# Two gathered tiles of each round, instead of one, fetched row by row by SyncE from byte offsets

## The chip, the core and the metric

One core of a Trainium2 chip. TensorE multiplies matrices, VectorE, ScalarE and GpSimd compute and copy, SyncE computes nothing and issues DMA transfers. The metric is the time of one execution on the device, in microseconds, median of the runs.

## The reference

A graph network layer on 12,500 nodes (128 values each) and 400,000 edges, sorted by their destination:

```python
h_nodes = mlp2(x);  h_edges = mlp2(edge_attr)                 # 64 wide
msg_in  = concatenate([h_nodes[dst], h_nodes[src], h_edges])  # per edge
msgs    = silu(msg_in @ msg_W1 + msg_b1) @ msg_W2 + msg_b2
agg     = segment_sum(msgs, dst) / maximum(counts, 1)
out     = layernorm(x + x + mlp2(concatenate([x, agg])))      # two norms in all
```

The part that matters here is `h_nodes[src]`: for each edge one row of 64 floats, at an index that the input gives.

## The kernel before

A first stage computes two tables of node rows in DRAM, `a_table` (the part of the first message layer that belongs to destinations) and `b_table` (sources), 256 bytes a row. It also keeps the nodes' hidden layer on chip (`nT`).

Then come 625 **units** of 640 edges, each 5 tiles of 128 edges. 25 units make a **round**, and there are 25 rounds; all of it is written out as straight code. For each unit TensorE adds up the first message layer in `p_pre`: `second_layer` (L696: edge part and destination part, against the window of `a_table` in `wa_ring`), then `source_term` (L702 adds the gathered rows in `b_ring`; L705 computes a tile from `colbuf`). ScalarE applies Silu, TensorE sums messages into a window of nodes (`window_sums`, L716), VectorE adds that to `agg`.

The source rows come in three ways. In 12 of the 25 units (`SPECIAL`) the fifth tile isn't gathered: VectorE and ScalarE copy 128 columns of `nT` into `colbuf` (L642), from lists of byte offsets made on chip (`column_bytes`, stored to DRAM by `store_column_bytes` and read back in pieces). GpSimd gathers the others with one indirect DMA for each tile of 128 rows (`pool_gathers`, L834), up to `BLAG` = 8 units ahead of TensorE: 112 tiles a round. The last tile is SyncE's: tile 3 of unit 24 (`ROW_TILE`), 128 transfers of one row each (`fetch_rows`, L763), 8 in each of units 7 to 22. For these SyncE loads 8 row numbers into registers (L758) from `row_list`, which is read from an input, and uses each as an index into `b_table`, an array of 4-byte floats 64 wide. Unit 24 has a slot of its own in `b_ring` (`b_slot`).

SyncE's program is `sync_units`, one queue in strict order. For unit i: at the first unit of a chunk (units 0, 5, 9, 13, 17, 21) a wait on `second_mm`, two edge loads (L809) and one of destinations (L811); the start of the unit's window, loaded 4 words at a time (`next_start`, L564); a wait for `second_mm`; the window of `a_table` (L815); at units 8 and 21 the column lists (L735); then the rows; then the loads and the store of the node update of the round before (L973, L974, L978). `second_mm` counts the units whose second layer is done, plus `LEAD` = 5, so that

```python
wait_alone(eng, second_mm, r * ROUND + i + 1)
```

lets SyncE go past the window of unit i when TensorE has finished the second layer of unit i - 5. TensorE needs a chunk's edges for `hidden_mm` (L849), which runs three units ahead: after the second layer of unit i it multiplies the edges of unit i + 3. It waits for the rows of unit 24 before that unit's source term.

Of the kernel before, what the change touches and what calls it, by code (L numbers as in the profile page):

```python
# [5 lines left out]
F32, I32, U8 = mybir.dt.float32, mybir.dt.int32, mybir.dt.uint8  # L6
ALU, ACT, AX = mybir.AluOpType, mybir.ActivationFunctionType, mybir.AxisListType
ds = bass.ds

P = 128  # L10
H = 64
D = 128
W = 64
TILES = 5
UE = TILES * P
HALF = UE // 2
ROUND = 25
# [22 lines left out]
LIST_AT = (21, 8)  # L40
LOAD = dict(vector=32, scalar=40)
LISTED = 656
ROW_TILE = (24, 3)
ROWS_A_STEP = 8
ROWS_FROM = 7
WORDS = 4

AT = dict(load=0, ready=2, count=3, mean=4, up=5, hidden=6, down=7, sum=8, norm1=9, affine=10, sum2=11, norm2=12,
# [10 lines left out]
def program(nc, a, out, stack):  # L59
# [25 lines left out]

    a_table = nc.dram_tensor("a_table", (NPAD, H), F32, kind="Internal").ap()
    b_table = nc.dram_tensor("b_table", (N, H), F32, kind="Internal").ap()
    byte_list = {who: nc.dram_tensor("bytes_for_" + who, (LISTED * LOAD[who],), I32, kind="Internal").ap() for who in COLS}
    assert all(LISTED >= UNITS + LEADIN + ROUND and LISTED * LOAD[who] % P == 0 for who in COLS)
    agg = sb("agg", [P, NPAD], F32)  # L90

# [39 lines left out]
    b_ring = sb("b_ring", [P, BRING, TILES, H], F32)  # L131
    wa_ring = sb("wa_ring", [P, RING, H], F32)
    hot_ring = sb("hot_ring", [P, HOTS, TILES, W], F32)
    all_cols = hot_ring[:, :, :, :].rearrange("p s t w -> p (s t w)").bitcast(I32)[:, 0:sum(LISTED * LOAD[who] // P for who in COLS)]
    comb = sb("comb", [P, COMBS, UE], F32)
    msg = sb("msg", [P, 2, TILES, H + 1], F32)
    work = sb("work", [P, 8 * BANK], F32)
# [8 lines left out]
    for who in COLS:  # L146
# [1 line left out]
        lists[who] = to_ab[0:1, :, :, :, :].rearrange("o s t q n -> o (s t q n)").bitcast(I32)[:, at:at + words]\  # L148
            .rearrange("o (k n) -> o k n", n=LOAD[who])
        at += words  # L150
    row_list = to_ab[0:1, :, :, :, :].rearrange("o s t q n -> o (s t q n)").bitcast(I32)[:, at:at + P]
    assert at + P <= SR * 2 * 2 * GJ * H
    pad = sb("pad", [W, H], F32)
    rows = e_ring[0:1, :, :].rearrange("p s c -> p (s c)")
    startf, ahead = rows[:, 0:UNITS], rows[:, UNITS:2 * UNITS]
# [190 lines left out]
    def scalar_nodes(eng):  # L346
        for to, of in first_fold:
            eng.dma_start(to, of).then_inc(s_wf, 16)
        eng.wait_ge(s_bx, 32)
        for k in range(PAIRS):  # L350
            if k < PAIRS:
                _, gs, n = pair_of[k]
                eng.wait_ge(s_h, k + 1)
                if k >= SR:
                    eng.wait_ge(s_ab, k - SR + 1)
                eng.activation(n1[k % SR][0:gs * H, 0:n].rearrange("k (j p) -> k j p", j=GJ),
                               p_hid[0:gs * H, k % 2, 0:n].rearrange("k (p j) -> k j p", j=GJ),
                               ACT.Silu, bias=b_n1[0:gs * H, :]).then_inc(s_n1, 1)
                first, _, _ = pair_of[k]
                for g in range(gs):  # L360
                    last = eng.activation(nT[:, first + g * n:first + (g + 1) * n], p_hid[g * H:(g + 1) * H, k % 2, 0:n],
                                          ACT.Silu, bias=b_n1[g * H:(g + 1) * H, :])
                last.then_inc(s_nt, 1)
            if k < len(fold_loads):
                to, of = fold_loads[k]
                eng.dma_start(to, of).then_inc(s_w, 16)
            if k == 5:
                eng.dma_start(dst[:, :], a["dst"]).then_inc(s_dst, 16)
            if k == PAIRS - 2:
                for who, words in column_parts():  # L370
                    eng.dma_start(words, a["cols_" + who]).then_inc(s_cols, 16)
        for to, of in later_loads:
            eng.dma_start(to, of).then_inc(s_w2, 16)

# [63 lines left out]
    def vector_nodes(eng):  # L438
# [21 lines left out]
            eng.tensor_copy(startf[:, :], first).then_inc(s_sf, 1)  # L460

        def column_bytes():
            eng.wait_ge(s_cols, 16 * len(COLS))
            eng.tensor_scalar(all_cols, all_cols, 4, None, ALU.mult).then_inc(s_byte, 1)

        def window_spread():

# [126 lines left out]
    def b_slot(i):  # L594
        return i % BLAG if i < ROUND - 1 else BLAG

    def gathered(i):

        return [k for k in range(TILES) if not (i in SPECIAL and k == TILES - 1)]

    def by_pool(i):

        return [k for k in gathered(i) if (i, k) != ROW_TILE]

    def b_value(r, i):

# [35 lines left out]
            end = copy(colbuf[:, special % COLBUF, at:at + 1].bitcast(U8), of[j])  # L642
        return end

    def column_parts():

        at = 0
        for who in COLS:
            words = LISTED * LOAD[who] // P
            yield who, all_cols[:, at:at + words]  # L650
            at += words

    def store_column_bytes(eng):
        eng.wait_ge(s_byte, 1)
        for who, words in column_parts():
            eng.dma_start(byte_list[who].rearrange("(p c) -> p c", p=P), words).then_inc(s_stl, 16)

    def a_value(r, i):
# [78 lines left out]

    def sync_first(eng):

        eng.wait_ge(s_stl, 16 * len(COLS))  # L740
        a_table_stored(eng)
        for i in range(SR):
            eng.wait_ge(s_stb[i], 16 * stores(PAIRS, i))
        load_list(eng, 0, 0, LEADIN, lead_in)
        load_list(eng, LEADIN, LEADIN, HALF_AT, list_in[0])

        load_rows(eng, 0)

    def load_rows(eng, r):

        eng.dma_start(row_list, a["rows"][ds(r * P, P)].unsqueeze(0)).then_inc(row_list_in, 16)

    def fetch_rows(eng, r, i):

        first = (i - ROWS_FROM) * ROWS_A_STEP
        if first == 0:
            wait_alone(eng, row_list_in, 16 * r + 16)
        _, nodes = nc.values_load_multi_w_load_instructions(  # L758
            row_list[:, first:first + ROWS_A_STEP], engines=[eng.engine], min_val=0, max_val=N - 1,
            skip_runtime_bounds_check_because="an edge's source is a node")  # L760
        unit, tile = ROW_TILE
        for q, node in enumerate(nodes):
            eng.dma_start(b_ring[first + q:first + q + 1, b_slot(unit), tile, :], b_table[ds(node, 1), :])\  # L763
               .then_inc(row_in[q % len(row_in)], 16)
        if first + ROWS_A_STEP == P:
            load_rows(eng, r + 1)

    def sync_last(eng):
# [28 lines left out]
    def sync_units(eng, base, n, step):  # L797
        for k in range(n):
            r, i = place(base, k)
            c, at = chunk_of(i)  # L800
            if at == 0:
                n = CHUNKS[c]
                first = r * (ROUND * UE) + i * UE
                here = slice(spot(i), spot(i) + n)

                wait_alone(eng, second_mm, r * ROUND + i + LEAD - CHUNKS[c - 1])
                cols = a["edgeT"][:, ds(first, n * UE)].rearrange("k (u c) -> k u c", c=UE)
                for part in range(2):
                    eng.dma_start(e_ring[part * H:(part + 1) * H, here, :], cols[:, :, part * HALF:(part + 1) * HALF])\  # L809
                       .then_inc(e_in[c % 2], 16)  # L810
                eng.dma_start(dst_ring[:, here, :].rearrange("p u c -> p (u c)"),  # L811
                              a["dst_row"][ds(first, n * UE)].partition_broadcast(H)).then_inc(d_in[c % 2], 16)
            start = next_start(eng, r, i)
            wait_alone(eng, second_mm, r * ROUND + i + 1)
            eng.dma_start(wa_ring[H:P, i % RING, :], a_table[ds(start, W), :]).then_inc(a_in[i % RING], 16)  # L815
            if i in LIST_AT:
                half = LIST_AT.index(i)
                copied = r * ROUND + LEADIN + (HALF_AT if half == 0 else 0)
                chunk, n = ((r + 1) * ROUND, HALF_AT) if half == 0 else (r * ROUND + HALF_AT, ROUND - HALF_AT)
                wait_alone(eng, col_ok["vector"], copied)  # L820
                wait_alone(eng, col_ok["scalar"], copied)
                load_list(eng, chunk + LEADIN, LEADIN + half * HALF_AT, n, list_in[half])
            if 0 <= i - ROWS_FROM < P // ROWS_A_STEP:
                fetch_rows(eng, r, i)
            step(k)

    def pool_gathers(eng, units):
# [24 lines left out]
    def tensor_units(eng, r, n, step):  # L852
# [14 lines left out]
        for i in range(n):  # L867
# [14 lines left out]
            if j in SPECIAL and i < ADD_LAG + 1:  # L882
                for who in COLS:
                    wait_alone(eng, col_ok[who], cols_value(who, rr, j))
            if j == ROW_TILE[0]:
                for arrived in row_in:
                    wait_alone(eng, arrived, (rr + 1) * (16 * P // len(row_in)))
            eng.wait_ge(b_in[b_slot(j)], b_value(rr, j))
            source_term(eng, i, j, b_slot(j)).then_inc(pre_mm, 1)
            step(i)  # L890
# [260 lines left out]
    with nc.Block() as block:  # L1151
# [34 lines left out]
        @block.vector  # L1186
        def _(eng):
            vector_nodes(eng)
            eng.sem_inc(sum_ok, 1)
            eng.sem_inc(gen["done"], 1)  # L1190
            eng.wait_ge(s_pool, 5)
            eng.wait_ge(s_stl, 16 * len(COLS))
            choose(eng, vector_first, vector_units, vector_general, vector_updates, vector_last)

def _laid_out(inputs):
# [9 lines left out]
    for k in ("src", "dst"):  # L1206
        d[k] = g[k].reshape(-1, P).T
    d["dst_row"] = g["dst"].reshape(-1)
    rows = g["src"].reshape(-1, ROUND, TILES, P)[:, ROW_TILE[0], ROW_TILE[1], :]
    d["rows"] = np.concatenate([rows, np.zeros_like(rows[0:1])]).reshape(-1)  # L1210
    special = g["src"].reshape(-1, ROUND, TILES, P)[:, SPECIAL, TILES - 1, :]
    chunks = special.shape[0] * ROUND
    for who, (first, last) in dict(vector=(0, COLS["vector"]), scalar=(COLS["vector"], P)).items():
# [2 lines left out]
        listed = np.zeros((LISTED, LOAD[who]), part.dtype)  # L1216
        for k in range(chunks):
            listed[k, 0:at[k + 1] - at[k]] = part[at[k]:at[k + 1]]
        d["cols_" + who] = listed.reshape(P, -1)
    return {k: np.ascontiguousarray(t) for k, t in d.items()}  # L1220

# [12 lines left out]
```

## Time and profile before

| | |
|---|---|
| time, median of 3 runs | 4890.29 us (4887.94 to 4896.6) |
| span of the profiled execution | 3612.0 us |
| median less span | 1278.3 us |
| units, from the first window load on SyncE to the last | 76 to 3552 us |
| GpSimd busy | 2674.4 us (74%) |
| ScalarE busy | 2994.3 us (83%) |
| TensorE matmuls busy | 2874.1 us (80%) |
| VectorE busy | 2737.3 us (76%) |

The page gives the profiled execution by its span from the first to the last instruction; the time of the runs holds 1278.3 us more, which the trace doesn't cover, so that a change in the span is set on the median as it is. A round takes (3552 - 76) / 25 = 139 us. Busy time doesn't hold what an engine's queue does with registers, loads into registers and issues of DMAs; SyncE has no busy time at all, and is read from its queue's instructions.

### The profile page before, as it was taken

What the parts mean: (1) busy time and instruction counts of PE and PEld (TensorE: products, weight loads), DVE (VectorE), ACT (ScalarE), POOL (GpSimd) and SP (SyncE); (2) the same over time, 40 slices, a digit from 0 to 9 for tenths busy, and PEclk for the clock granted to TensorE, in tenths of its full rate; (3) what the DMA queues carried; (4) which work ended last, traced back from release to release, by engine and by line L of the source; (5) the groups of instructions that cost most, each with busy time, mean ns of one, the idle gap of its engine ahead of it and who ended that gap; (6) DMA issues with size and microseconds to landing.
All of it is one profiled execution on the core that took longest, in us unless ns stands there. A gap on an engine that the chain in (4) does not pass through costs nothing.

```text
span 3612.0 us, 103943 instructions
## 1 busy us (share of the span) xinstructions
PE 2874.1 (80%) x16224; PEld 2219.4 (61%) x16224; DVE 2737.3 (76%) x20847; ACT 2994.3 (83%) x23073; POOL 2674.4 (74%) x2823
## 2 busy tenths in 40 slices
PE   4878888877878878888778888777778878877885
PEld 2666666666666666666666666656665656656664
DVE  4777778778777777777787777787777777877876
ACT  4998888888887888988888888888878888888785
POOL 4777777777777777777777777777777777777773
PEclk7687777677777777777777777777777776677766
DMA  7454444454444454444454444444444444444441
GB/s 225 78 113 100 87 94 100 89 102 96 95 95 86 96 102 90 101 100 88 93 103 85 102 96 95 99 95 87 98 92 99 101 89 96 90 92 102 96 95 43
DMA packets 263059, 350.77 MB, mean 97 GB/s; under 512 B 111714, under 2 KB 199121, under 8 KB 252514
## 3 DMA queue, kind: packets, MB, share of 16 engines
q1 hardware_dynamic: 169792, 246.77, 32.0%
q0 software_dynamic: 90624, 95.15, 14.5%
q14 instruction: 558, 4.57, 0.5%
q8 instruction: 131, 2.15, 0.3%
q10 hardware_dynamic: 1954, 2.14, 0.2%
HBM read 330.78 MB, written 13.01 MB: 95 GB/s over the span
## 4 chain that ended last, share of the span: by engine, by line
POOL 62%; issue 21%; PE 8%; DMA 4%; DVE 4%; DVEq 0%; ACT 0%; SPq 0%; ACTq 0%; POOLq 0%
POOL b_ring L834 62%; DMA b_ring<-b_table,src 4%; PE p_pre L696 2%; PE p_pre L702 1%; DVE colbuf L642 1%; PE p_sum L716 1%; PE p_hid L849 1%; DVE comb L939 1%; DMA work<-in_xT 1%; PE p_pre L705 0%; PE p_last L995 0%; PE p_last L996 0%; DVEq L627 0%; DVE stats L1032 0%; ACT colbuf L642 0%
## 5 line engine op out<-in xcount | busy, mean ns | idle before, releaser
L834 POOL DMA_INDIRECT b_ring<-b_table,src x2800 | 2652.0, 947 | 858.9 <-issue 844.8
L642 ACT COPY colbuf<-shared 64x4 uint8 x21134 | 2127.4, 190 | 159.9 <-issue 148.4
L642 DVE COPY colbuf<-shared 64x4 uint8 x17511 | 1377.6, 194 | 308.6 <-issue 301.9
L696 PE MATMUL p_pre<-wa_ring,comb 128*128 128x64 f32 x6250 | 1047.1, 329 | 0.0
L696 PEld LDWEIGHTS p_pre<-wa_ring,comb 128*128 128x128 f32 x6250 | 996.8, 245 | 0.9 <-issue 0.8
L727 ACT ACTIVATE comb<-p_hid,b_e 64x320 f32<-64x320 f32 x1250 | 652.8, 522 | 360.4 <-PE p_hid L849 350.9
L939 DVE SCALAR_TENSOR_TENSOR comb<-shared,p_const 64x640 f32<-64x640 int32 x625 | 554.0, 887 | 458.8 <-PE p_pre L696 336.2
L716 PEld LDWEIGHTS p_sum<-hot_ring,msg 128*65 128x65 f32 x6250 | 589.2, 181 | 500.0 <-DVE agg L949 265.0
L716 PE MATMUL p_sum<-hot_ring,msg 128*65 128x64 f32 x6250 | 649.5, 269 | 291.1 <-DVE agg L949 166.6
L702 PE MATMUL p_pre<-b_ring,ident 128*128 128x320 f32 (+1 forms) x1250 | 583.4, 559 | 341.4 <-DMA b_ring<-b_table,src 340.8
L849 PE MATMUL p_hid<-e_ring,w_e 128*128 128x320 f32 x1250 | 626.2, 591 | 49.0 <-DMA e_ring<-in_edgeT 40.0
L702 PEld LDWEIGHTS p_pre<-b_ring,ident 128*128 128x128 f32 x1250 | 302.1, 255 | 559.7 <-DMA b_ring<-b_table,src 439.9
L928 DVE TENSOR_TENSOR hot_ring<-dst,p_const 128x320 f32<-128x320 f32 x625 | 304.7, 487 | 19.7
L721 ACT ACTIVATE msg<-p_pre 128x320 f32<-128x320 f32 x625 | 273.6, 438 | 22.8 <-PE p_pre L702 12.8
L849 PEld LDWEIGHTS p_hid<-e_ring,w_e 128*128 128x128 f32 x1250 | 245.9, 244 | 54.3 <-DMA e_ring<-in_edgeT 44.1
L705 PEld LDWEIGHTS p_pre<-w_ab,colbuf 64*128 64x128 f32 x600 | 111.6, 232 | 137.4 <-issue 137.4
L705 PE MATMUL p_pre<-w_ab,colbuf 64*128 64x64 f32 x600 | 158.6, 353 | 0.0
L949 DVE TENSOR_TENSOR agg<-agg,p_sum 65x64 f32 x625 | 135.4, 217 | 9.0 <-issue 3.4
L1022 DVE RECIPROCAL p_last<-p_last 64x500 f32<-64x500 f32 x25 | 82.1, 3282 | 0.9
L1001 PEld LDWEIGHTS p_last<-w_u,work 65*125 65x125 f32 x200 | 49.1, 321 | 6.1 <-ACT work L1006 2.4
L995 PE MATMUL p_last<-work,w_ux 128*64 128x500 f32 x50 | 45.8, 1016 | 5.3 <-DVE work L1024 5.3
L1001 PE MATMUL p_last<-w_u,work 65*125 65x128 f32 x200 | 47.6, 388 | 0.8 <-ACT work L1006 0.8
(106 smaller groups left out, 599.2 us busy)
## 6 DMA issues: line engine op xcount, KB each, us to landing
e_ring<-in_edgeT SPq DMA_DIRECT2D x250, 320.0 KB
shared<-in_dst_row SPq DMA_DIRECT2D x125, 640.0 KB
b_ring<-b_table SPq DMA_DIRECT2D x3200, 0.2 KB
b_ring<-b_table,src POOLq DMA_INDIRECT x2800
e_ring<-in_edgeT SPq DMA_DIRECT2D x50, 400.0 KB
shared<-in_dst_row SPq DMA_DIRECT2D x25, 800.0 KB
wa_ring<-a_table SPq DMA_DIRECT2D x625, 16.0 KB
work<-in_xT SPq DMA_DIRECT2D x25, 250.0 KB
```

Source lines behind the costliest of these rows:

```text
L642: end = copy(colbuf[:, special % COLBUF, at:at + 1].bitcast(U8), of[j])
L696: return eng.matmul(p_pre[:, i % 2, k * H:(k + 1) * H], comb[:, i % COMBS, k * P:(k + 1) * P], wa_ring[:, i % RING, :], start=k == 0, stop ...
L702: last = eng.matmul(p_pre[:, i % 2, 0:n * H], ident[:, :], b_ring[:, slot, 0:n, :].rearrange("p k n -> p (k n)"), start=False, stop=n == T ...
L705: last = eng.matmul(p_pre[:, i % 2, n * H:(n + 1) * H], colbuf[:, SPECIAL.index(j) % COLBUF, :], w_ab[0:H, H:2 * H], start=False, stop=True)
L716: last = eng.matmul(sums_of(i), msg[:, i % 2, k, :], hot_ring[:, i % HOTS, k, :], start=k == 0, stop=k == TILES - 1)
L721: return eng.activation(msg[:, i % 2, :, 0:H], of, ACT.Silu)
L727: last = eng.activation(comb[0:H, i % COMBS, part * HALF:(part + 1) * HALF], p_hid[rows, bank, 0:HALF], ACT.Silu, bias=b_e1[rows, :])
L834: eng.indirect_dma_start(b_ring[:, b_slot(i), k, :], None, b_table, bass.IndirectOffsetOnAxis(ap=src[:, u * TILES + k:u * TILES + k + 1], ...
L849: eng.matmul(p_hid[:, i % 2, 0:HALF], w_e1[:, :], e_ring[:, spot(j), :], start=True, stop=True)\
L928: eng.tensor_tensor(hot_ring[:, i % HOTS, :, :], dst[:, ds((base + i) * TILES, TILES)].bitcast(F32).unsqueeze(2).to_broadcast([P, TILES, W ...
L939: eng.scalar_tensor_tensor(comb[H:P, i % COMBS, :], dst_ring[:, spot(j), :], win_from[:, ds(base + i, 1)], p_row.to_broadcast([H, UE]), AL ...
L949: eng.tensor_tensor(window, window, sums_of(i), ALU.add).then_inc(sum_ok, 1)
```

## The change

Tile 2 of unit 24 is fetched by SyncE too (`ROW_TILES`), so GpSimd gathers 111 tiles a round instead of 112. SyncE fetches 256 rows a round: 12 in each of units 5 to 20, 16 in each of units 21 to 24. Their offsets come as bytes: the list of row numbers is multiplied by 256 on VectorE in the first stage, together with the column lists, stored to DRAM and read back 256 words a round. The source of a transfer is now a slice of `b_table` seen as single bytes. The loads into registers (now 12 or 16 words) stand ahead of the wait for `second_mm` instead of behind the window's load.

```diff
-ROW_TILE = (24, 3)
-ROWS_A_STEP = 8
-ROWS_FROM = 7
+ROW_TILES = [(24, 2), (24, 3)]
+ROWS = P * len(ROW_TILES)
+ROWS_FROM = 5
+ROWS_A_STEP = [12] * 16 + [16] * 4
...
+            eng.tensor_scalar(all_lists[:, columns:], all_lists[:, columns:], 4 * H, None, ALU.mult).then_inc(s_byte, 1)
...
-        return [k for k in gathered(i) if (i, k) != ROW_TILE]
+        return [k for k in gathered(i) if (i, k) not in ROW_TILES]
...
-        eng.dma_start(row_list, a["rows"][ds(r * P, P)].unsqueeze(0)).then_inc(row_list_in, 16)
-
-    def fetch_rows(eng, r, i):
-
-        first = (i - ROWS_FROM) * ROWS_A_STEP
+        eng.dma_start(row_list, byte_list["rows"][ds(r * ROWS, ROWS)].unsqueeze(0)).then_inc(row_list_in, 16)
+
+    def row_numbers(eng, r, i):
+
+        k = i - ROWS_FROM
+        first, n = sum(ROWS_A_STEP[0:k]), ROWS_A_STEP[k]
         if first == 0:
             wait_alone(eng, row_list_in, 16 * r + 16)
-        _, nodes = nc.values_load_multi_w_load_instructions(
-            row_list[:, first:first + ROWS_A_STEP], engines=[eng.engine], min_val=0, max_val=N - 1,
+        _, starts = nc.values_load_multi_w_load_instructions(
+            row_list[:, first:first + n], engines=[eng.engine], min_val=0, max_val=4 * H * (N - 1),
             skip_runtime_bounds_check_because="an edge's source is a node")
-        unit, tile = ROW_TILE
-        for q, node in enumerate(nodes):
-            eng.dma_start(b_ring[first + q:first + q + 1, b_slot(unit), tile, :], b_table[ds(node, 1), :])\
+        return starts
+
+    def fetch_rows(eng, r, i, starts):
+
+        first = sum(ROWS_A_STEP[0:i - ROWS_FROM])
+        for q, start in enumerate(starts):
+            which, row = divmod(first + q, P)
+            unit, tile = ROW_TILES[which]
+            eng.dma_start(b_ring[row:row + 1, b_slot(unit), tile, :].bitcast(U8), b_bytes[ds(start, 4 * H)].unsqueeze(0))\
                .then_inc(row_in[q % len(row_in)], 16)
-        if first + ROWS_A_STEP == P:
+        if first + len(starts) == ROWS:
             load_rows(eng, r + 1)
...
             start = next_start(eng, r, i)
+            fetches = 0 <= i - ROWS_FROM < len(ROWS_A_STEP)
+            starts = row_numbers(eng, r, i) if fetches else None
             wait_alone(eng, second_mm, r * ROUND + i + 1)
```

## Rows read from the trace of the kernel before

**Rows 1.** The page: its head and the busy time of the engines.
```profile
span 3612.0 us, 103943 instructions
...
PE 2874.1 (80%) x16224; PEld 2219.4 (61%) x16224; DVE 2737.3 (76%) x20847; ACT 2994.3 (83%) x23073; POOL 2674.4 (74%) x2823
```
**Rows 2.** The page's costliest groups: GpSimd's gathers.
```profile
L834 POOL DMA_INDIRECT b_ring<-b_table,src x2800 | 2652.0, 947 | 858.9 <-issue 844.8
```
**Rows 3.** Who waited for whom: us in total, times, longest us.
```profile
POOL b_ring L834 <- issue: 844.8, 2772, 0.3
...
PE p_pre L702 <- DMA b_ring<-b_table,src: 340.8, 141, 6.6
...
PE p_hid L849 <- DMA e_ring<-in_edgeT: 40.0, 25, 11.7
...
POOL b_ring L834 <- PE p_pre L705: 5.2, 17, 0.3
```
**Rows 4.** The same for SyncE's queue.
```profile
SPq L815 <- PE p_pre L696: 755.6, 229, 12.7
SPq L558 <- PE p_pre L696: 88.4, 23, 6.2
```
**Rows 5.** Single lines on SyncE: duration in ns, min/median/max, first and last start.
```profile
L763 SPq FUSED_REGOPS  x3200: 37/37/42, 104.8 to 3545.1; - x189
L763 SPq MOVE b_ring<-b_table x3200: 29/29/38, 104.9 to 3545.1; - x189
L763 SPq DMA_DIRECT2D b_ring<-b_table x3200: 217/225/327, 105.0 to 3545.2; - x189
...
L758 SPq TENSOR_LOAD <-to_ab x400: 524/962/983, 104.3 to 3541.2; - x134
...
L564 SPq TENSOR_LOAD <-win_start x157: 303/603/1697, 75.4 to 3547.0; - x157
...
L815 SPq DMA_DIRECT2D wa_ring<-a_table x625: 468/486/547, 76.4 to 3551.9; - x157
```
**Rows 6.** A single line on VectorE's queue: the load of 28 words into registers.
```profile
L627 DVEq TENSOR_LOAD <-to_ab x633: 850/1850/3725, 73.6 to 3570.5; - x159
```
**Rows 7.** SyncE's timeline, cut to four row transfers, then two units (start, us, what).
```profile
1131.06 1.45 SPq L763 DMA_DIRECT2D b_ring<-b_table  x4
...
1129.79 3.13 SPq L763 DMA_DIRECT2D b_ring<-b_table  x8
1133.10 0.49 SPq L815 DMA_DIRECT2D wa_ring<-a_table  x1
...
1134.76 3.12 SPq L763 DMA_DIRECT2D b_ring<-b_table  x8
```
**Rows 8.** The timelines of SyncE and TensorE around the chunk of unit 13.
```profile
2502.70 1.33 SPq L809 DMA_DIRECT2D e_ring<-in_edgeT  x2
2504.07 0.61 SPq L811 DMA_DIRECT2D shared<-in_dst_row  x1
...
2508.41 0.81 PE L849 MATMUL p_hid<-e_ring,w_e 128*128 128x320 f32 x2
```
**Rows 9.** TensorE's timeline: second layers of units 22, 24, 25; two, elsewhere, apart.
```profile
2578.37 2.32 PE L696 MATMUL p_pre<-wa_ring,comb 128*128 128x64 f32 x10
...
2589.64 1.28 PE L696 MATMUL p_pre<-wa_ring,comb 128*128 128x64 f32 x10
...
2592.51 1.28 PE L696 MATMUL p_pre<-wa_ring,comb 128*128 128x64 f32 x10
...
695.57 2.34 PE L696 MATMUL p_pre<-wa_ring,comb 128*128 128x64 f32 x10
...
701.64 2.34 PE L696 MATMUL p_pre<-wa_ring,comb 128*128 128x64 f32 x10
```
**Rows 10.** SyncE's timeline: the shortest and a long one of the other issues.
```profile
1017.22 0.24 SPq L751 DMA_DIRECT2D to_ab<-in_rows  x1
...
1051.15 0.58 SPq L973 DMA_DIRECT2D work<-in_xT  x1
```

More of the change, by code:

```diff
@@ L87, in program @@
     b_table = nc.dram_tensor("b_table", (N, H), F32, kind="Internal").ap()
-    byte_list = {who: nc.dram_tensor("bytes_for_" + who, (LISTED * LOAD[who],), I32, kind="Internal").ap() for who in COLS}
+    byte_list = {"rows": nc.dram_tensor("bytes_for_rows", ((E // UE // ROUND + 1) * ROWS,), I32, kind="Internal").ap()}
+    byte_list |= {who: nc.dram_tensor("bytes_for_" + who, (LISTED * LOAD[who],), I32, kind="Internal").ap() for who in COLS}
     assert all(LISTED >= UNITS + LEADIN + ROUND and LISTED * LOAD[who] % P == 0 for who in COLS)
@@ L133, in program @@
     hot_ring = sb("hot_ring", [P, HOTS, TILES, W], F32)
-    all_cols = hot_ring[:, :, :, :].rearrange("p s t w -> p (s t w)").bitcast(I32)[:, 0:sum(LISTED * LOAD[who] // P for who in COLS)]
+    listed = {who: LISTED * LOAD[who] // P for who in COLS} | {"rows": (ROUNDS + 1) * ROWS // P}
+    all_lists = hot_ring[:, :, :, :].rearrange("p s t w -> p (s t w)").bitcast(I32)[:, 0:sum(listed.values())]
+    assert sum(ROWS_A_STEP) == ROWS and ROWS_FROM + len(ROWS_A_STEP) <= ROUND
+    b_bytes = b_table.rearrange("n h -> (n h)").bitcast(U8)
     comb = sb("comb", [P, COMBS, UE], F32)
@@ L150, in program @@
         at += words
-    row_list = to_ab[0:1, :, :, :, :].rearrange("o s t q n -> o (s t q n)").bitcast(I32)[:, at:at + P]
-    assert at + P <= SR * 2 * 2 * GJ * H
+    row_list = to_ab[0:1, :, :, :, :].rearrange("o s t q n -> o (s t q n)").bitcast(I32)[:, at:at + ROWS]
+    assert at + ROWS <= SR * 2 * 2 * GJ * H
     pad = sb("pad", [W, H], F32)
@@ L369, in scalar_nodes @@
             if k == PAIRS - 2:
-                for who, words in column_parts():
-                    eng.dma_start(words, a["cols_" + who]).then_inc(s_cols, 16)
+                for who, words in list_parts():
+                    eng.dma_start(words, a["list_" + who]).then_inc(s_cols, 16)
         for to, of in later_loads:
@@ L462, in column_bytes @@
         def column_bytes():
-            eng.wait_ge(s_cols, 16 * len(COLS))
-            eng.tensor_scalar(all_cols, all_cols, 4, None, ALU.mult).then_inc(s_byte, 1)
+            eng.wait_ge(s_cols, 16 * len(listed))
+            columns = sum(listed[who] for who in COLS)
+            eng.tensor_scalar(all_lists[:, 0:columns], all_lists[:, 0:columns], 4, None, ALU.mult).then_inc(s_byte, 1)
+            eng.tensor_scalar(all_lists[:, columns:], all_lists[:, columns:], 4 * H, None, ALU.mult).then_inc(s_byte, 1)
         def window_spread():
@@ L643, in copied_columns, with list_parts @@
         return end
-    def column_parts():
+    def list_parts():
         at = 0
-        for who in COLS:
-            words = LISTED * LOAD[who] // P
-            yield who, all_cols[:, at:at + words]
+        for who, words in listed.items():
+            yield who, all_lists[:, at:at + words]
             at += words
     def store_column_bytes(eng):
-        eng.wait_ge(s_byte, 1)
-        for who, words in column_parts():
+        eng.wait_ge(s_byte, 2)
+        for who, words in list_parts():
             eng.dma_start(byte_list[who].rearrange("(p c) -> p c", p=P), words).then_inc(s_stl, 16)
@@ L738, in sync_first @@
     def sync_first(eng):
-        eng.wait_ge(s_stl, 16 * len(COLS))
+        eng.wait_ge(s_stl, 16 * len(listed))
         a_table_stored(eng)
@@ L822, in sync_units @@
                 load_list(eng, chunk + LEADIN, LEADIN + half * HALF_AT, n, list_in[half])
-            if 0 <= i - ROWS_FROM < P // ROWS_A_STEP:
-                fetch_rows(eng, r, i)
+            if fetches:
+                fetch_rows(eng, r, i, starts)
             step(k)
@@ L884, in tensor_units @@
                     wait_alone(eng, col_ok[who], cols_value(who, rr, j))
-            if j == ROW_TILE[0]:
+            if j == ROW_TILES[0][0]:
                 for arrived in row_in:
-                    wait_alone(eng, arrived, (rr + 1) * (16 * P // len(row_in)))
+                    wait_alone(eng, arrived, (rr + 1) * (16 * ROWS // len(row_in)))
             eng.wait_ge(b_in[b_slot(j)], b_value(rr, j))
@@ L1191, in _ @@
             eng.wait_ge(s_pool, 5)
-            eng.wait_ge(s_stl, 16 * len(COLS))
+            eng.wait_ge(s_stl, 16 * len(listed))
             choose(eng, vector_first, vector_units, vector_general, vector_updates, vector_last)
@@ L1208, in _laid_out @@
     d["dst_row"] = g["dst"].reshape(-1)
-    rows = g["src"].reshape(-1, ROUND, TILES, P)[:, ROW_TILE[0], ROW_TILE[1], :]
-    d["rows"] = np.concatenate([rows, np.zeros_like(rows[0:1])]).reshape(-1)
+    tiles = g["src"].reshape(-1, ROUND, TILES, P)
+    rows = np.concatenate([tiles[:, unit, tile, :] for unit, tile in ROW_TILES], axis=1)
+    d["list_rows"] = np.concatenate([rows, np.zeros_like(rows[0:1])]).reshape(P, -1)
     special = g["src"].reshape(-1, ROUND, TILES, P)[:, SPECIAL, TILES - 1, :]
@@ L1218, in _laid_out @@
             listed[k, 0:at[k + 1] - at[k]] = part[at[k]:at[k + 1]]
-        d["cols_" + who] = listed.reshape(P, -1)
+        d["list_" + who] = listed.reshape(P, -1)
     return {k: np.ascontiguousarray(t) for k, t in d.items()}
```

## The prediction

> **What bounds the kernel now.** I read the page first. No engine is busy above 83% [rows 1], so busy shares don't name the bound. The costliest groups do: GpSimd's 2800 gathers are busy for 2652.0 us, and 844.8 us of idle time lie between them, all put down to issue [rows 2]. Each gather so takes (2652.0 + 844.8) / 2800 = 1.249 us, and 112 of them make 139.9 us, the whole round. The waits confirm it: of the 2800, GpSimd waited 17 times for the last product of a unit, 5.2 us in total, while TensorE waited 340.8 us for gathered tiles [rows 3]. GpSimd never stops, and the others follow it.
>
> Then I looked at the engine that gets the work. SyncE waits for TensorE at L815 in only 229 of 625 units, 755.6 us, and 88.4 us at L558 [rows 4]. Of the 3476 us from its first to its last window load it is thus occupied for 3476 - 844 = 2632 us, 105.3 us of each round, and it has 34.6 us to spare. In 396 units it finds its condition met, that is, it comes late; the two neighbouring units of the timeline begin their rows 4.97 us apart [rows 7] without any slack, where GpSimd's pace is 139.9 / 25 = 5.60 us a unit.
>
> **What the change takes from GpSimd.** One gather a round: 1.249 us, 25 times, 31 us. A round on GpSimd alone would be 111 x 1.249 = 138.6 us. This is all that can be gained.
>
> **What one row costs on SyncE.** Four transfers in a run end 1.45 us after the first begins; less the last one's 0.225 us, the pitch is 1.225 / 3 = 0.408 us [rows 5, 7]. It holds three instructions: FUSED_REGOPS 37 ns, MOVE 29 ns, the transfer 225 ns; 117 ns are left, three gaps of 39 ns. Bounds: 0.254 us if all the gaps went with it, 0.371 us if only the 37 ns go, 0.408 us if nothing does. Rows a round: 128 x 0.408 = 52.2 us now, 256 x 0.332 = 85.0 us after.
>
> The Trainium skill ("DMA: Bandwidth & Descriptors", section "Anatomy of one DMA") gives about 50 ns for the dispatch of a DMA by the sequencer; the trace has 225 ns. By the page's figure, estimated, a row would cost 0.157 us, SyncE would keep up, and the change would be worth its 31 us.
>
> **What the loads into registers cost.** Eight words take 962 ns in the median and 524 ns at least [rows 5]; 28 words on VectorE take 1850 ns [rows 6]. That is 0.044 to 0.066 us for each further word. Some loads will stand right behind another one and be short. I take 1.10 us for 12 words and 1.35 us for 16, with a gap of 0.04 us: 1.14 and 1.39 us. Bounds: 0.524 us (no growth) and 1.85 us. Their place ahead of the wait hides them only where SyncE waits.
>
> **SyncE's sum alone.** Now 105.3; less 52.2 for rows and 16 x 1.00 for loads; plus 85.0, 16 x 1.14 and 4 x 1.39: 145.9 us. Already this is above 139.9.
>
> **The chain of one round.** SyncE can't spread this sum over the round. In units 0 to 4 it has no rows and is soon held by `second_mm`. So I follow it from the moment when TensorE's second layer of unit 0 lets it past the wait of unit 5:
> - 256 rows: 85.0
> - loads, 15 of 12 words (that of unit 5 lies ahead of the wait) and 4 of 16: 17.1 + 5.6 = 22.7
> - 20 window loads, each 486 + 29 + 37 ns and three gaps of 40: 13.4
> - the chunks of units 9, 13, 17, 21 and of the next unit 0, each 2.02 (1.98 from first to last, and a gap) [rows 8]: 10.1
> - 5 loads of window starts of 0.603 + 0.04 [rows 5]: 3.2
> - eight short issues (four of column lists, one of offsets, three of the node update), 0.24 to 0.58 us each [rows 10], about 0.38 with the gap: 3.0
>
> Together 137.4 us, back to back. 20 units of GpSimd's pace are 112 us, so SyncE falls behind by 25 us. What is late next is the chunk of the next unit 0: TensorE needs its edges three units ahead, right after the second layer of unit 22, and VectorE its destinations. They land 3.7 us after the last issue: in the trace the product with new edges starts at 2508.41, SyncE's issues end at 2504.68 [rows 8], and this is an upper bound there. Then TensorE has to do units 23, 24 and 0 up to the second layer before SyncE is let past the wait of unit 5 again: 2592.51 - 2578.37 = 14.1 us for three such steps [rows 9]. Bounds: 3 x 2.87 = 8.6 us at the pace of the last step of these, 3 x 6.07 = 18.2 us at that of the slow pair. The release itself is 0.2 us.
>
> Round: 137.4 + 3.7 + 14.1 + 0.2 = 155.4 us, against 139.9: 15.5 us more, 25 times, 387 us. The span becomes about 4000 us; the 1278 us around it stay, and the median 4890 becomes 5277 us.
>
> Free, and why: the offsets' product on VectorE and one more list to store are under 1 us once, beside two stores of the same kind. The rows of unit 24 are issued before the late chunk, and TensorE needs them almost two units after it. Slots: eight units of GpSimd's lead are 45 us, more than the 25 us by which TensorE falls behind, so GpSimd only waits.
>
> **The rivals.**
> - *GpSimd stays the bound (the other side).* If SyncE's chain fits in 138.6 us, the round shrinks by 1.25 us: 4859 us. This decides at one price, the pitch: 0.332 - 16.8 / 256 = 0.266 us. For it: three gaps might shrink together, and the bound of 0.254 lies below. Against: it wants MOVE or the transfer shorter as well, and the transfer's 217 to 225 ns hardly vary [rows 5]. 10%; a pitch near 0.271 would give no change, 3%.
> - *SyncE bounds by its sum only.* If the light units hid what I charge for landing and for TensorE's three steps, the round is 145.9 us: +150 us, 5040 us. For it: TensorE comes through 2.87 us steps. Against: the wait at L815 is in the code. 9%.
> - *Loads don't grow with their words.* 19 of them at 0.524 + 0.04 make 10.7 instead of 22.7 us: round 143.4, +88 us, 4978 us. Against: 1850 ns for 28 words [rows 6]. 5%. The Trainium skill (same page, "Latency and other measured facts") gives a floor of some 600 ns for such a load, amortized by taking several words. At 0.64 us each, an estimate, the round would be 144.9 us and the time 5015 us; the trace's 962 ns speaks against it.
> - *Byte transfers save nothing.* At 0.408 the round is 155.4 + 19.5 = 174.9 us: 5765 us; at 0.371, 5527 us. For it: no transfer of single bytes from DRAM is in this trace. Against: FUSED_REGOPS only stands where an index is multiplied. 7%.
>
> **How the numbers follow.** The forecast has 66%: 5277 us, by TensorE's bounds 5140 to 5380, so with its own range 5100 to 5420. The range for 8 in 10 takes in the second and third rival and leaves out the first and the last (10 + 3 + 7 = 20%): 4980 to 5480. Faster by over 0.2% (10 us, about what a measurement tells from no change) 10%, within it 3%, slower 87%.
>
> **What the changed profile would show.** No FUSED_REGOPS at the line of the rows, and runs of transfers with a pitch of 0.33 us. Loads of about 1.1 and 1.35 us. SyncE waiting in three or four units a round, those without rows, instead of nine. GpSimd no longer without waits: 25 x (155.4 - 138.6) = 420 us behind the last product of a unit. TensorE waiting for edges or VectorE for destinations once a round, near unit 22, for 10 us or more. Wrong it would be with a pitch below 0.27 us, with GpSimd still at 1.249 us without waits, or with a stall in another place: rows of unit 24 that come last, or a chunk in the middle of the rows.

## The result, and the profile after

The changed kernel took 5552.77 us (5546.78 to 5558.01, 4 runs) against 4889.11 us, a ratio of 1.1365 (95% interval 1.1338 to 1.1392): 664 us slower, where 387 were forecast, and outside the range.

The page of the changed kernel shows at once what the forecast had missed. Its head, the engines' busy time, the gathers:

```profile
span 5549.8 us, 107221 instructions
...
PE 3422.5 (62%) x16224; PEld 2655.8 (48%) x16224; DVE 2933.4 (53%) x20848; ACT 3124.7 (56%) x23073; POOL 2662.0 (48%) x2798
...
L849 POOL DMA_INDIRECT b_ring<-b_table,src x2775 | 2639.6, 951 | 2772.0 <-PE p_pre L708 1456.4
```

This execution's own time is 5551.7 us: span and time differ by 2 us, and so they did in every later run of either kernel. So 1278 us of "time around the span" never existed. The page of the kernel before, with 3612 us [rows 1], must have come from an execution that was itself some 1276 us shorter than the timed ones. All runs since then fall on two levels, and each set of runs, made one after the other, has only one of them: the medians of the kernel before are 3611 to 3614 us in some sets and 4884 to 4952 us in others, with nothing between. The first comparison was made at the longer level, its forecast from a profile of the shorter one. I call the two conditions A (about 3611 us) and B (about 4900 us) from here on. They aren't two kinds of chip, though the expectations below speak so: the sets recorded under chip number 10 were in A at first, in B 20 minutes later, and in A again after that.

What B does shows most plainly on SyncE's queue. Single lines on it in the changed kernel in B (duration min/median/max in ns), and two runs of 12 rows among many from its timeline:

```profile
L776 SPq MOVE b_ring<-b_table x6400: 2/29/1422, 129.6 to 5510.6; - x194
L776 SPq DMA_DIRECT2D b_ring<-b_table x6400: 3/225/963, 129.7 to 5510.7; - x194
...
2589.06 3.91 SPq L776 DMA_DIRECT2D b_ring<-b_table  x12
...
2594.76 7.10 SPq L776 DMA_DIRECT2D b_ring<-b_table  x12
```

FUSED_REGOPS is gone from the line of the rows, as forecast, and the medians of the rest are those of [rows 5]. But a MOVE that took 29 to 38 ns now takes between 2 and 1422 ns, and of two runs of 12 transfers one takes 3.91 us and the next 7.10. The queue is held up, mostly for 0.6 to 0.8 us at a time, and then does a few instructions in a few ns each.

The same kernel in A, with nothing held up: single lines, the queue's waits, GpSimd's wait.

```profile
L776 SPq MOVE b_ring<-b_table x6400: 29/29/38, 100.2 to 4039.8; - x194
L776 SPq DMA_DIRECT2D b_ring<-b_table x6400: 217/225/433, 100.3 to 4039.8; - x194
...
L765 SPq TENSOR_LOAD <-to_ab x500: 748/1013/3137, 87.0 to 4032.8; - x167
...
SPq L830 <- PE p_pre L702: 311.5, 65, 11.8
...
POOL b_ring L849 <- PE p_pre L708: 461.4, 91, 14.2
```

Here it took 4080.5 us against 3613.4 (ratio 1.1294, 1.127 to 1.1317): 467 us slower. SyncE waits at L830 in 65 units of 625 instead of 229 [rows 4], GpSimd waits 461 us for the product at L708, where its waits for the last product of a unit had been 5.2 us in all [rows 3].

### The profile page after: what moved, and what is told of

Read it like the earlier page. It is cut to its first block, busy times and chain, and to the rows that moved or that the text cites. A ratio compares the mean times of both kernels' runs of the same rounds, so it can differ in the third digit from the quotient of the medians.

```text
span 5549.8 us, 107221 instructions
## 1 busy us (share of the span) xinstructions
PE 3422.5 (62%) x16224; PEld 2655.8 (48%) x16224; DVE 2933.4 (53%) x20848; ACT 3124.7 (56%) x23073; POOL 2662.0 (48%) x2798
## 4 chain that ended last, share of the span: by engine, by line
SPq 54%; issue 30%; DVE 6%; DMA 4%; PE 3%; another core or an unknown queue 2%; DVEq 1%; ACT 0%; ACTq 0%
SPq L776 36%; SPq L765 7%; SPq L830 5%; DVE colbuf L649 4%; DMA shared<-in_dst_row 3%; SPq L822 2%; DVE comb L954 1%; PE p_pre L702 1%; SPq L571 1%; SPq L824 1%; DMA e_ring<-in_edgeT 1%; PE p_sum L722 1%; DVEq L634 1%; SPq L741 0%
## 5 line engine op out<-in xcount | busy, mean ns | idle before, releaser
L649 ACT COPY colbuf<-shared 64x4 uint8 x21134 | 2252.0, 190 | 821.6 <-issue 801.8
L649 DVE COPY colbuf<-shared 64x4 uint8 x17511 | 1533.3, 193 | 974.8 <-issue 964.8
L864 PE MATMUL p_hid<-e_ring,w_e 128*128 128x320 f32 x1250 | 768.0, 712 | 1025.0 <-DMA e_ring<-in_edgeT 988.8
L722 PE MATMUL p_sum<-hot_ring,msg 128*65 128x64 f32 x6250 | 750.7, 296 | 1043.6 <-DVE agg L964 423.4
L722 PEld LDWEIGHTS p_sum<-hot_ring,msg 128*65 128x65 f32 x6250 | 672.3, 206 | 1330.7 <-DVE agg L964 833.5
L702 PE MATMUL p_pre<-wa_ring,comb 128*128 128x64 f32 x6250 | 1277.3, 380 | 0.0
L702 PEld LDWEIGHTS p_pre<-wa_ring,comb 128*128 128x128 f32 x6250 | 1224.7, 294 | 1.0 <-issue 1.0
L864 PEld LDWEIGHTS p_hid<-e_ring,w_e 128*128 128x128 f32 x1250 | 295.1, 291 | 1048.6 <-DMA e_ring<-in_edgeT 1010.9
L708 PE MATMUL p_pre<-b_ring,ident 128*128 128x320 f32 (+1 forms) x1250 | 653.2, 621 | 1.0 <-DMA b_ring<-b_table 1.0
L708 PEld LDWEIGHTS p_pre<-b_ring,ident 128*128 128x128 f32 x1250 | 373.8, 299 | 208.1 <-issue 182.6
```

The source lines that it names most:

```text
L702: return eng.matmul(p_pre[:, i % 2, k * H:(k + 1) * H], comb[:, i % COMBS, k * P:(k + 1) * P], wa_ring[:, i % RING, :], start=k == 0, stop ...
L708: last = eng.matmul(p_pre[:, i % 2, 0:n * H], ident[:, :], b_ring[:, slot, 0:n, :].rearrange("p k n -> p (k n)"), start=False, stop=n == T ...
L722: last = eng.matmul(sums_of(i), msg[:, i % 2, k, :], hot_ring[:, i % HOTS, k, :], start=k == 0, stop=k == TILES - 1)
L864: eng.matmul(p_hid[:, i % 2, 0:HALF], w_e1[:, :], e_ring[:, spot(j), :], start=True, stop=True)\
```

## The experiments

**The kernel before, again, and the two halves of the change apart.** `one_tile_bytes` sets, in the changed kernel,

```diff
-ROW_TILES = [(24, 2), (24, 3)]
-ROWS_FROM = 5
-ROWS_A_STEP = [12] * 16 + [16] * 4
+ROW_TILES = [(24, 3)]
+ROWS_FROM = 7
+ROWS_A_STEP = [8] * 16
```

and `two_tiles_index` keeps two tiles but goes back to the old address, `b_table[ds(start, 1), :]`, with the list multiplied by 1. (The letters of the theories below are those of the expectations, not the two conditions.)

> The kernel before, unchanged. Its profiled execution spanned 3612 us, while its runs took 4889; in the changed kernel span and time differ by 2 us only. Theory A (what SyncE's instructions cost by the first trace): the span is 3612 us again and some 1278 us lie around it, which the change removed in an unknown way. Theory B (SyncE stalls while it issues single-row transfers, and the first trace of the kernel before happened to show an execution almost without stalls): the span is about 4885 us, and the runs of eight rows take well over 3.1 us.

> The changed kernel with one tile on SyncE, 8 rows in each of units 7 to 22 as before, but from byte offsets and with the loads ahead of the wait. Theory A: GpSimd bounds, no change from before (4889, within 10 us). Theory B, SyncE is the bound already and each row costs its instructions plus a stall: 128 x 76 ns x 25 = 243 us faster (4646) if the stall is added to the instructions; no change if the stall is a rate at which rows are taken, whatever the instructions.

> The changed kernel, but with row numbers as indices (256 rows by the old form of address, the product back in front of each transfer). Theory A: 256 x 76 ns x 25 = 486 us slower than the changed kernel, 6040. Theory B with a rate at which rows are taken: the product hides in the stall, 5550 to 5600.

The set was an A: the kernel before took 3611.08 us, its repeat 3614.49 with a span of 3612.7. Neither theory had foreseen that: the span came back as in A, but nothing lay around it, and the time had fallen to it. One tile by bytes: 3612.86 us, ratio 1.0006 (0.9996 to 1.0015). Two tiles by index: 4618.76 us, 1.2781 (1.2756 to 1.2807). So the byte form with the loads ahead of the wait changes nothing while GpSimd bounds, and the second tile on SyncE costs over 1000 us in the old form. The changed kernel, measured in a later set of A at 4080.5 us, is 538 us below that, where 486 were expected: 538 / (256 x 25) = 0.084 us a row. Runs of rows from the timelines of the one tile by bytes and of the two tiles by index:

```profile
1128.35 2.64 SPq L776 DMA_DIRECT2D b_ring<-b_table  x8
```

```profile
2303.24 4.79 SPq L776 DMA_DIRECT2D b_ring<-b_table  x12
```

Eight rows take 2.64 us where [rows 7] have 3.12 to 3.13, that is 0.06 to 0.07 us less a row; (4.79 - 0.225) / 11 = 0.415 us a row by index.

**The changed kernel again, and three of its terms.** The set was a B. `chunk_ahead` moves three transfers on SyncE, those of the next round's first chunk, now in a function `load_chunk` (cut):

```diff
+            if early and i == ROUND - 1 and k + 1 < UNITS:
+                load_chunk(eng, r + 1, 0)
             if fetches:
                 fetch_rows(eng, r, i, starts)
```

`loads_once` calls `row_numbers` at unit 5 only and uses its registers for the whole round; it leaves out the offsets of the other rows, and so fetches the same 12 again and again. `tile_left_out` is `one_tile_bytes`, with the slot of the missing tile set to zero once and

```diff
-        return [k for k in gathered(i) if (i, k) not in ROW_TILES]
+        return [k for k in gathered(i) if (i, k) not in ROW_TILES + [(24, 2)]]
```

> The changed kernel itself, on the chip where the kernel before takes 3611 us and two tiles by index take 4619. Theory A (SyncE's chain by what its instructions take, pitch 0.332 us): 3611 + 387 = 3998 us; or, taken from the measured index form less 256 x 76 ns x 25 = 486 us, 4133 us. Theory B (stalls between the row transfers belong to two tiles on SyncE and come back on any chip): 5550 us, with pitches of 0.5 us and more in the runs of rows. If A holds, the first comparison (4889 to 5553) was made in a condition of the chip that slows SyncE's queue in both kernels.

> The changed kernel, with the edges and destinations of the next round's first chunk issued before the 16 rows of unit 24 instead of behind them. Theory A (the chunk behind the rows is what TensorE waits for once a round, and it hands the lateness on): the chain loses the 16 rows, 16 x 0.332 = 5.3 us a round, 133 us faster than the changed kernel. Theory C (SyncE's plain sum bounds, the order on it doesn't matter): no change.

> The changed kernel, but the offsets are loaded into registers once a round, at unit 5, and used again by the steps behind it, so that the rows fetched are mostly others than the edges': 19 loads a round are left out, all transfers stay. Theory A: the chain loses 22.7 us a round and fits under GpSimd's 138.6: 3580 us. Theory C (plain sum, 145.9 - 22.7 = 123): also 3580. Theory D (the loads are short or hidden, the transfers are the cost): at most 90 us faster than the changed kernel.

> One tile on SyncE by byte offsets, 8 rows a step as before, and tile 2 of unit 24 fetched by nobody (its slot is set to zero once): GpSimd does 111 gathers a round, SyncE 128 rows. It shows what taking the gather from GpSimd is worth when SyncE pays nothing. GpSimd bounds: 25 x 1.249 = 31 us faster than before, 3580 us. If something else binds as soon as GpSimd gives way: 3611.

Beside 4951.93 us for the kernel before: the changed kernel 5639.21 (1.1386, 1.135 to 1.1423), chunk ahead 5498.7, loads once 5236.44, tile left out 4648.41 (0.9381, 0.9362 to 0.9401). The chunk's place is worth 141 us (133 expected). The other two are far off what theory A gives: in B neither the loads' 403 us nor the 304 us of the last one can be read as instruction times. The last one holds two changes, moreover: the last experiment below shows that its one tile in byte form is 5% faster in B without leaving a tile out, so that most of its 6% isn't the gather's. My theory B (a stall that belongs to two tiles on SyncE) fell too, since the kernel before, with one tile, had itself gone from 3611 to 4952 us.

**The kernel before in B.**

> The kernel before once more, for its trace where this call's chip takes about 4900 us for it. Two levels have been seen for it, 3611 and 4890 to 4952 us. In the changed kernel's slow trace SyncE's queue has some 3,500 records of under 20 ns and about 1,450 holes of 0.6 to 0.8 us; the first trace of before has 80 and 10. Theory E (the levels are a condition of the chip that holds up SyncE's queue, whatever the kernel): at 4900 us this trace shows the holes too, and a span within 5 us of its time; at 3611 us it shows none.

> The changed kernel once more. If the kernel before takes 3611 us beside it: theory A, the chain by what instructions take, 3998 us, or 4133 us by way of the measured index form; a row's pitch of 0.332 us; one wait of TensorE for edges a round. If the kernel before takes 4900 beside it: 5550 to 5640 again.

Again a B: 4949.6 us, and 5634.16 for the changed kernel (1.1391, 1.1357 to 1.1425). The traced execution of the kernel before took 4959.05 us. Its span and the line of the rows, and two runs of its timeline (the view ends within the second, after seven of its eight transfers):

```profile
span 4957.1 us, 103943 instructions
...
L763 SPq FUSED_REGOPS  x3200: 3/37/1412, 146.4 to 4895.8; - x189
L763 SPq MOVE b_ring<-b_table x3200: 2/29/1413, 146.5 to 4895.9; - x189
L763 SPq DMA_DIRECT2D b_ring<-b_table x3200: 2/225/1438, 146.6 to 4895.9; - x189
...
2518.49 3.13 SPq L763 DMA_DIRECT2D b_ring<-b_table  x8
...
2523.46 6.66 SPq L763 DMA_DIRECT2D b_ring<-b_table  x7
```

Against [rows 5] the medians are the same and the extremes are not. Theory E holds: the hold-ups belong to the condition and meet both kernels.

They don't meet SyncE alone. These are idle stretches of VectorE and ScalarE put down to "issue", in which they waited for nothing that the profile shows, first in A, then in B, and GpSimd's waits in B:

```profile
DVE colbuf L642 <- issue: 301.9, 483, 4.8
...
ACT colbuf L642 <- issue: 148.4, 254, 21.5
```

```profile
DVE colbuf L642 <- issue: 976.9, 1537, 8.6
...
ACT colbuf L642 <- issue: 874.9, 1528, 25.1
...
POOL b_ring L834 <- PE p_pre L702: 808.9, 245, 24.6
...
POOL b_ring L834 <- PE p_pre L705: 304.8, 154, 8.5
```

Counted in the two traces of the kernel before, stretches of 0.5 us and more between two instructions of one queue, where the second has no semaphore to wait for: none in A; 1,204 on SyncE, 878 on VectorE and 749 on ScalarE in B. And GpSimd, which never stopped in A, now waits over 1100 us for TensorE's products: in B it isn't the bound.

**The chain in A.**

> The changed kernel, hoping for a chip that takes 3611 us for the kernel before (there the index form was measured, with 180.4 us a round, and the byte form with one tile, with a pitch of 0.318 us). Theory A, undisturbed: 180.4 - 256 x 0.090 = 157.4 us a round, 3611 + 25 x 17.5 = 4049 us; SyncE waits at units 3, 4 and 5 of a round and TensorE for edges at unit 22. On a chip that takes 4950 us for the kernel before: 5630 again.

> The changed kernel with 16 rows in each of units 5 to 20 and none in 21 to 24: the same 256 rows, three loads a round fewer, done earlier. Theory A (the chain: SyncE's work from unit 5 on, then TensorE's way from the chunk that comes late to the next release): now the last late chunk is that of unit 21, and TensorE has seven units to do from there instead of three, at some 4.7 us, while SyncE's chain is 11 us shorter: a round 19 - 11 = 8 us longer, 200 us slower than the changed kernel. Theory C (SyncE's plain sum): three loads fewer, 75 us faster.

> One tile by byte offsets, the loads ahead of the wait, 8 rows a step. On a chip that takes 3611 us for the kernel before it was the same (ratio 1.0006). On one that takes 4950: Theory E (SyncE's queue is held up there, and then it bounds the kernel before too): fewer instructions a row make it faster, by 128 x 0.09 us x 25 = 288 us or more, to 4660, near the 4648 of the kernel that leaves a tile out. If GpSimd bounds there: 4950.

An A: the kernel before 3613.4 us, the changed kernel 4080.5 (4049 expected), 16 rows in 16 units 4247.8 (1.1754, 1.1734 to 1.1774), one tile by bytes 3611.21 (0.9996). `rows_16` is one line, `ROWS_A_STEP = [16] * 16`. It has fewer loads and is 167 us slower, where the plain sum promised 75 us faster and the chain 200 slower. Its SyncE waits at L830 in 131 units, twice as many as the 65 of the changed kernel:

```profile
SPq L830 <- PE p_pre L702: 438.0, 131, 11.5
```

**The loads and the chunk in A, and one tile by bytes in B.**

> The changed kernel with the offsets loaded once a round and used again, so that most rows fetched are others than the edges': 19 loads a round left out. Undisturbed the changed kernel takes 4080 us and a load of 12 words about 1.0 us. Theory A: 19 loads and their gaps, about 20 us a round, leave the chain: 158.4 - 20 = 138.4, GpSimd's pace: 3580 to 3620 us. If the chain keeps part of it elsewhere: above 3650. Held up (before at 4950): 5236 again.

> The changed kernel with the next round's first chunk ahead of the 16 rows of unit 24. Theory A: the chunk comes 16 x 0.318 = 5.1 us earlier, 127 us faster than 4080: 3953. Theory C (plain sum): 4080. Held up it was 5499 against 5639.

> One tile by byte offsets, once more, for a chip that takes 4950 us for the kernel before: 4660 if SyncE's queue bounds there, 4950 if not. On a chip at 3613: 3611.

An A, with 3614.05 us for the kernel before: loads once 3583.18 us (0.9914, 0.9897 to 0.993), chunk ahead 3947.34 (3953 expected), one tile 3610.79. With 19 of its 20 loads gone the kernel with 256 row transfers a round is faster than before by 31 us, the whole worth of the gather that GpSimd gave up. Its gathers and GpSimd's wait for TensorE:

```profile
L851 POOL DMA_INDIRECT b_ring<-b_table,src x2775 | 2627.9, 947 | 851.6 <-issue 833.5
...
POOL b_ring L851 <- PE p_pre L708: 6.1, 20, 0.3
```

2775 gathers at (2627.9 + 833.5) / 2775 = 1.247 us, without a pause: GpSimd bounds again.

> One tile by byte offsets, for a chip that takes 4950 us for the kernel before: 4660 if SyncE's queue bounds there, 4950 if not. On a chip at 3613: 3611, as three times before.

A B: 4633.04 us against 4883.81 (0.9495, 0.9467 to 0.9524), by 251 us, with 288 or more expected. There less work on SyncE makes the kernel faster, as it doesn't in A. What the missing product and what the earlier place of the loads has of it wasn't taken apart.

## Why the prediction was wrong

**The step that failed** is the last of the sum: "The span becomes about 4000 us; the 1278 us around it stay, and the median 4890 becomes 5277 us." A span of 3612 beside a time of 4889 was no constant to carry along but the sign that profile and timed runs were made in different conditions. So the terms of the sum were sized in A and applied in B. The term that is too small there is SyncE's work: the change adds 40.6 us a round by the forecast (105.3 to 145.9), 40.4 in A, but 49.2 in B.

This is by the forecast's own measure: from the first to the last start of a window load, over 25 rounds, and less the waits. For B, these rows are of the kernel before and of the changed kernel, both from the second B set:

```profile
L815 SPq DMA_DIRECT2D wa_ring<-a_table x625: 3/480/782, 89.8 to 4899.2; - x157
...
SPq L815 <- remote: 880.4, 146, 10.7
...
SPq L558 <- remote: 43.9, 19, 5.1
...
SPq L815 <- PE p_pre L696: 35.3, 15, 16.9
```

```profile
L830 SPq DMA_DIRECT2D wa_ring<-a_table x625: 3/486/964, 92.3 to 5577.0; - x157
...
SPq L830 <- remote: 246.1, 26, 10.9
SPq L830 <- PE p_pre L702: 160.1, 29, 15.4
```

("remote" stands where the profile can name no releaser on the core.) The rows for A are [rows 4], [rows 5] and, of the changed kernel, 80.9 to 4034.0 us at L830 with the 311.5 us of waits shown above. Each figure is rounded by itself.

| SyncE, us a round | A: before | A: changed | B: before | B: changed |
|---|---|---|---|---|
| occupied | 105.3 | 145.7 | 154.0 | 203.1 |
| waiting for TensorE | 33.8 | 12.5 | 38.4 | 16.2 |
| sum | 139.0 | 158.1 | 192.4 | 219.4 |

The time that SyncE gives up in waits is nearly the same in both, 21 and 22 us; what differs is how long the added work takes. The medians of that B set differ by 684.6 us, 27.4 a round. The forecast had 15.5; 3.2 more were missing in A already (below), and 8.8 are hold-ups on the added work. Together that is 27.5. In the first comparison the medians differ by 663.7 us, 26.5 a round.

The forecast's first step fails in B as well: GpSimd bounds the kernel before only in A. That adding 387 to a wrong base came out as near as it did, 5277 for 5553, is partly luck: base and change were taken from two conditions.

**In A the chain was right.** One round of the changed kernel in A, in SyncE's timeline (from the release at unit 5 to the next) and TensorE's:

```profile
1682.85 0.52 SPq L830 DMA_DIRECT2D wa_ring<-a_table  x1
...
1814.29 5.23 SPq L776 DMA_DIRECT2D b_ring<-b_table  x16
...
1820.19 1.36 SPq L822 DMA_DIRECT2D e_ring<-in_edgeT  x2
1821.60 0.61 SPq L824 DMA_DIRECT2D shared<-in_dst_row  x1
...
1841.30 0.52 SPq L830 DMA_DIRECT2D wa_ring<-a_table  x1
```

```profile
1827.02 1.44 PE L864 MATMUL p_hid<-e_ring,w_e 128*128 128x320 f32 x2 [18.54 <-DMA e_ring<-in_edgeT]
...
1839.85 1.28 PE L702 MATMUL p_pre<-wa_ring,comb 128*128 128x64 f32 x10
```

Read it as one path. SyncE works from 1682.85 to 1822.21 without a wait (the five window loads behind that, from 1822.41 on, are the light units); TensorE has stood for 18.54 us when the edges come at 1827.02; it does three units up to the end of the second layer of unit 0 at 1841.13; 0.17 us later SyncE is let past the wait of unit 5.

| a round, us | forecast | this one |
|---|---|---|
| SyncE back to back | 137.4 | 139.4 |
| landing of the late chunk | 3.7 | 4.8 |
| TensorE's three steps | 14.1 | 14.1 |
| release | 0.2 | 0.2 |
| sum | 155.4 | 158.5 |

- *Cost of a row:* 16 transfers in 5.23 us are (5.23 - 0.225) / 15 = 0.334 us each; forecast 0.332. Right, and with it that MOVE stays.
- *Loads:* median 1013 ns for 12 and 16 words together; forecast 1.10 and 1.35 us. Leaving out 19 of 20 took 497 us off in A (4080.5 to 3583.18, in two sets whose kernels before agree within 1 us), 19.9 us a round, where 22.7 were charged and the gain ends at GpSimd's pace.
- *Late chunk:* right; moving it ahead of 16 rows gave 133 us, 16 x 0.334 x 25 = 134.
- *Gain from GpSimd:* 31 us forecast, 31 us measured in A as soon as SyncE's chain was short enough.
- *Total in A:* +387 forecast, +467 measured, 3.2 us a round more. Landing and the two further us on SyncE's side are 3.1 of these 3.2 us; the landing had been read from a product that shows no wait of its own [rows 8], and wasn't the upper bound that I took it for.
- *Rivals:* "by its sum only" is refuted by `rows_16` and `chunk_ahead`, "loads don't grow" by the loads' 748 ns at the least, "byte transfers save nothing" by the pitch. "GpSimd stays the bound" would have needed a row of 0.266 us. It came true in A only when 19.9 us a round of loads were gone.

**The figures of the Trainium skill.** The 50 ns of dispatch stand in a section of "DMA: Bandwidth & Descriptors" whose full title is "Anatomy of one DMA — SWDGE (gpsimd) path": it is about DMAs that GpSimd issues, and the prediction set its figure against SyncE's transfers. By it the kernel would have been faster by 31 us. The trace keeps 225 ns a transfer on SyncE with or without the product in front of it, so the figure isn't to be used for this queue. The floor of some 600 ns for a load into registers (same page, "Latency and other measured facts") isn't undercut by 12 to 16 words here, 748 ns at least and 1013 in the median in A; but loads of 4 words took 303 ns at least [rows 5], half of it.

**What stays open** is the cause of the hold-ups in B. The runs show that they go with a set of runs and not with the kernel or the chip's number, that they meet SyncE, VectorE and ScalarE, and that medians don't show them. The traces name no releaser for them. The DMA engines' own work doesn't get longer: the packets of queue q1, which has most of the traffic, took 32.0% of 3612.0 us in A, 1156 us, and 23.0% of 4957.1 us in B, 1140 us. TensorE's mean granted clock is lower in B, 0.605 against 0.745 in the changed kernel. A slower TensorE doesn't account for a MOVE of 1.4 us, which waits for no engine; whether the hold-ups lower the clock, or both have a third cause, wasn't tried. Nor was it taken apart how much of B's longer time comes from SyncE's hold-ups and how much from those of the other two; SyncE's alone are 48.7 of the 53.4 us by which a round of the kernel before is longer.

No kernel here is shown to be faster than the kernel before in both conditions while it does all the work. One tile by byte offsets is equal to the kernel before in A (three sets, ratios 0.9992 to 1.0006) and 5% faster in B. It is the version to keep.

## What to carry to other kernels

When the profiled span and the timed runs of one kernel differ by a quarter, find out why before making any sum; a forecast on a wrong baseline is right only by luck. Work that is handed to an in-order queue costs more than its own sum where the queue also carries loads with a due time: follow the chain from the last release to the late transfer and through the consumer to the next release, and put the transfers with a due time ahead of the bulk. Here 128 further transfers of 0.33 us, and longer loads with them, bought one gather of 1.25 us.

## What the runs showed of the hardware

- In some sets of runs the queues of SyncE, VectorE and ScalarE are held up, SyncE's mostly for 0.6 to 0.8 us at a time (MOVE 2 to 1422 ns, against 29 to 38), and the same program takes about 4900 us instead of 3611. One and the same chip number showed both. Among the sets of the shorter level the medians of the kernel before agree within 0.1%.
- A transfer of one row of 256 bytes from a register address holds SyncE for 0.33 us from byte offsets and 0.41 from an index, in long runs; the transfer itself is 225 ns in both.
- A load of 12 to 16 words into registers takes SyncE about as long as three such transfers, 1013 ns in the median.
